# Spreading the maxima of an attention layer over its heads, with stacks of their own, and moving the FFN's low parts to GpSimd

## What is computed

```python
xn = _layernorm(x, axis=-1)
x = x + attn(xn, W_qkv, W_out, rel_emb) + ffn(xn, router_w, w1, b1, w2, b2)

# attn: 16 heads of 16
scores = jnp.einsum('bhqd,bhkd->bhqk', q, k)
scores = scores + compute_bias(rel_emb, S, S)      # bucketed relative position
attn = jax.nn.softmax(scores, axis=-1)
out = jnp.einsum('bhqk,bhkd->bhqd', attn, v)       # then @ W_out

# ffn: F = 1024; top-2 router probabilities, normalised, summed
expert_out = gelu(xt @ w1 + b1) @ w2 + b2
out = expert_out * jnp.sum(combine, axis=-1, keepdims=True)
```

## Time and profile before

| | |
|---|---|
| median of three runs | 3269.54 us (3268.29 to 3270.3) |
| the profiled execution | 3269.68 us, its span 3267.8 us |
| busy: PE, VectorE, ScalarE, GpSimd | 98%, 86%, 75%, 40% |
| chain that ended last: PE, VectorE, DMA | 77%, 3%, 2% |
| stage 1, up to the start of attention | 0 to 594 us |
| attention | 594 to 3199 us |
| projection | 3202 to 3268 us |

### The profile page before, as it was taken

The page is one execution under the profiler, slowest core; times in us unless marked ns, Lnnn a source line. Parts: engine busy times, 40 slices in busy tenths (PEclk is TensorE's granted clock), DMA queues, the critical chain, the costliest instruction groups (busy, mean ns, idle before and its releaser), DMA issues.

```text
span 3267.8 us, 72368 instructions
## 1 busy us (share of the span) xinstructions
PE 3200.7 (98%) x28170; PEld 1717.4 (53%) x28170; DVE 2813.3 (86%) x3760; ACT 2439.0 (75%) x4667; POOL 1297.9 (40%) x1918
## 2 busy tenths in 40 slices
PE   7999999799999999999999999999999999999997
PEld 6888889344444444444444444444444444444446
DVE  5577765699999999999999999999999999999922
ACT  4443344588888888888888888888888888888883
POOL 1212112344444444444444444444444444444445
PEclk9999999899999999999999999999999999999999
DMA  8532232432222222221122222212222221222105
GB/s 194 123 91 78 78 108 87 78 66 37 37 37 37 37 37 37 37 37 37 37 37 37 37 37 37 37 37 37 37 37 37 37 37 37 37 37 37 23 10 186
DMA packets 136725, 175.46 MB, mean 54 GB/s; under 512 B 53008, under 2 KB 100816, under 8 KB 130048
## 3 DMA queue, kind: packets, MB, share of 16 engines
q1 hardware_dynamic: 136384, 170.83, 25.6%
HBM read 110.31 MB, written 56.69 MB: 51 GB/s over the span
## 4 chain that ended last, share of the span: by engine, by line
PE 77%; DVE 3%; DMA 2%; issue 1%; SPq 0%; POOL 0%; ACT 0%; DVEq 0%; ACTq 0%
PE ps L1108 27%; PE ps L1125 24%; PE ps L1097 18%; PE ps L1130 8%; DVE max_half L1042 2%; DMA out_rows<-base_in 1%; PE ps L1165 0%; DMA k_st<-base_in 0%; DMA base_in<-base_rows 0%; SPq L194 0%; POOL prob L1007 0%; DVE neg_turn L1055 0%; SPq L860 0%; POOL turned L1015 0%; ACT turned L967 0%
## 5 line engine op out<-in xcount | busy, mean ns | idle before, releaser
L1042 DVE TENSOR_REDUCE max_half<-ps 128x1 f32<-128x512 f32 (+1 forms) x2666 | 2398.1, 945 | 121.5 <-PE ps L1097 118.1
L960 ACT ACTIVATE prob<-ps 128x512 f32<-128x512 f32 x4096 | 2156.3, 600 | 440.4 <-PE ps L1108 428.4
L1007 POOL TENSOR_TENSOR prob<-prob,near 128x224 f32<-128x224 f32 (+2 forms) x1664 | 978.3, 603 | 1450.9 <-ACT prob L960 1444.6
L1108 PE MATMUL ps<-q_st,k_st 49*128 49x512 f32 x4096 | 1407.3, 442 | 21.4 <-DMA k_st<-base_in 21.1
L1097 PE MATMUL ps<-k_st,q_st 48*128 48x512 f32 x3968 | 1403.2, 450 | 8.5 <-DVE max_half L1042 7.1
L1108 PEld LDWEIGHTS ps<-q_st,k_st 49*128 49x128 f32 x4096 | 658.8, 184 | 747.3 <-ACT prob L960 681.1
L1125 PE MATMUL ps<-prob,vr 128*32 128x384 f32 x4864 | 756.3, 498 | 0.0
L1097 PEld LDWEIGHTS ps<-k_st,q_st 48*128 48x128 f32 x3968 | 636.9, 184 | 180.7 <-DVE max_half L1042 103.3
L1125 PE MATMUL ps<-prob,vx 128*32 128x384 f32 x3328 | 593.5, 499 | 1.1 <-issue 1.1
L1125 PEld LDWEIGHTS ps<-prob,vr 128*32 128x32 f32 x4864 | 133.4, 108 | 325.5 <-issue 221.4
L662 PE MATMUL ps<-xnt,w_parts 128*128 128x512 f32 x1152 | 275.4, 398 | 8.7 <-DVE parts L512 5.1
(11 more groups left out here) (70 smaller groups left out, 1161.6 us busy)
## 6 DMA issues: line engine op xcount, KB each, us to landing
qk_parts<-parts SPq DMA_DIRECT2D x64, 512.0 KB, 4.7
q_st<-qk_parts SPq DMA_DIRECT2D x192, 128.0 KB, 3.9
k_st<-qk_parts SPq DMA_DIRECT2D x192, 128.0 KB, 5.4
near<-bias_near SPq DMA_DIRECT2D x64, 352.0 KB, 6.2
x_sb<-in_L_attn_hidden_states SPq DMA_DIRECT2D x18, 512.0 KB, 6.1
base_rows<-x_sb SPq DMA_DIRECT2D x16, 512.0 KB, 2.9
recip_rows<-recip_all SPq DMA_DIRECT2D x256, 32.0 KB, 1.8
base_in<-base_rows SPq DMA_DIRECT2D x16, 512.0 KB, 5.7
```

The costliest lines, as they stand in the source:

```text
L960: nc.scalar.activation(prob[:, t % PROBS, CH * j:CH * (j + 1)], ps[:, bank_of(at)], ACT.Exp).then_inc(drained, 1)
L1007: nc.gpsimd.tensor_tensor(at, at, near[n % GROUP][:, side, c0:c0 + q1 - q0], ALU.mult).then_inc(near_done, 1)
L1042: nc.vector.tensor_reduce(max_half[:, m % 2].rearrange("p i c -> p (i c)")[:, k:k + len(banks)], tiles, AX.X, ALU.max) \
L1108: nc.tensor.matmul(ps[:, bank_of(at)], k_st[u][:, P * kb:P * (kb + 1)], q_st[u][:, CH * c:CH * (c + 1)], start=True, stop=True).then_inc(s ...
```

## The change

Four things are changed.

1. **The stream of maxima.** The 62 heads' 3968 tiles are no longer tied to "two heads ahead, one for each score tile". `max_groups` spreads them evenly over the 4010 tile places of heads 0 to 62 (without the last 8 visits of head 62). A visit takes as many as the running share says: mostly as many as it has score tiles, in 42 visits one fewer. The maxima of head m so end at visit 22, 44, 66 ... and later by and by: for head 41 at visit 9 of head 40, for head 63 at visit 13 of head 62. `combine` comes one visit later and `turn` two visits later. Scores use 3 banks to the end.
2. **Stacks.** There are two for scores and two for maxima. Q and K of a head are loaded twice: `load(n+1)` at the start of head n, `load_max(m)` after the maxima of head m - 2. SyncE's queue for a head has a new order.
3. **Early pieces.** All 64 are in batch 1, 16 in each chunk: 3 in the QK part, 4 in F1, 1 in VR, 8 in F2, these last in banks 4 and 5.
4. **FFN low parts** are made by GpSimd (`hid_lows`), with `norm` ahead of the fourth of them and `exps` behind the eighth.

```diff
+VISIT_OF = [v for v, visit in enumerate(VISITS) for _ in visit]
+SPARE = 8
...
 def max_groups():
...
+    wanted, slots = CPB * KB * (NH - EARLY_HEADS), CPB * KB * (NH - 1) - sum(len(visit) for visit in VISITS[NV - SPARE:])
+    passed = done = 0
+    for t in range(NV * NH):
+        passed = min(passed + len(VISITS[t % NV]), slots)
+        take = wanted * passed // slots - done
+        tiles = []
+        while take > 0:
+            m, k = EARLY_HEADS + done // (CPB * KB), done % (CPB * KB)
+            size = min(take, 2, CPB * KB - k)
...
+            if k + size == CPB * KB:
+                ends[m] = t, at
...
+TURN_LATER = 2
...
+                def hid_lows(n):
+                    for f in range(KF):
+                        if f == 3:
+                            norm(n + 1)
+
+                        wait(pool, hid_high, KF * n + f + 1)
+                        if f == 0:
+                            wait(pool, f2_ready, TPC * n)
+                        nc.gpsimd.tensor_tensor(hid[:, 1, f], hid_raw[:, f % RAWS], hid[:, 0, f].bitcast(F32), ALU.subtract).then_inc(hid_low, 1)
...
-                for b in range(1, B - 1):
+                for b in range(1, B):
                     for c in range(CPB):
-                        chunk(b, c, early=True)
-                for c in range(CPB):
-                    chunk(B - 1, c, last=c == CPB - 1)
+                        chunk(b, c, early=b <= EARLY_PASSES, last=b == B - 1 and c == CPB - 1)
...
+                def load_max(m):
+
+                    if m - STACKS >= EARLY_HEADS:
+                        sp.wait_ge(max_ready, max_end(m - STACKS))
+                    load_stacks(sp, m, q_max[m % STACKS], k_max[m % STACKS], max_in[m % STACKS])
+
+                def load_maxima(first, last):
+
+                    for m in range(EARLY_HEADS + STACKS, NH):
+                        if first <= MAX_ENDS[m - STACKS][0] < last:
+                            load_max(m)
...
+                def turned_in(n):
+
+                    return MAX_ENDS[n][0] + TURN_LATER if n >= EARLY_HEADS else 0
+
                 def shift(n):
 
-                    wait(sp, neg_turned, n + 1)
+                    wait(sp, score_ready, CPB * KB * (n - STACKS + 1))
+                    sp.wait_ge(neg_turned, n + 1)
...
                 for n in range(NH):
-                    if n + GROUP - 1 < NH:
-                        load(n + GROUP - 1)
-                        load_near(n + GROUP - 1)
+                    early_turn = n + 1 < NH and turned_in(n + 1) < NV * n
                     if n + 1 < NH:
+                        load(n + 1)
+                    if early_turn:
                         shift(n + 1)
+                    load_maxima(NV * (n - 1) + NORM_AT, NV * n)
+                    if n + NEARS - 1 < NH:
+                        load_near(n + NEARS - 1)
                     if n > 0:
                         totals(n - 1)
                         spread(n - 1)
+                    load_maxima(NV * n, NV * n + TOTAL_AT)
+                    if n > 0:
                         keep(n - 1)
+                    load_maxima(NV * n + TOTAL_AT, NV * n + NORM_AT)
+                    if n + 1 < NH and not early_turn:
+                        shift(n + 1)
```

More of the change, by code:

```diff
@@ L132 @@
 NEAR_UP_TO = [sum(len(visit_parts(visit)) for visit in VISITS[:v]) for v in range(NV + 1)]
+VISIT_OF = [v for v, visit in enumerate(VISITS) for _ in visit]
+SPARE = 8
 def max_groups():
     freed = {bank: bank - CPB for bank in range(CPB)}
[L138 to L156, removed]
+    groups, order, in_visit, ends = [], {}, [], {}
+    wanted, slots = CPB * KB * (NH - EARLY_HEADS), CPB * KB * (NH - 1) - sum(len(visit) for visit in VISITS[NV - SPARE:])
[7 more added lines that the diff above has]
+            size = min(take, 2, CPB * KB - k)
+            at = len(groups)
+            choices = [range(bank, bank + size) for bank in range(CPB + 1 - size)]
+            banks = min(choices, key=lambda taken: sorted((freed[bank] for bank in taken), reverse=True))
+            for i in sorted(range(size), key=lambda i: freed[banks[i]]):
+                tiles.append((m, k + i, banks[i], freed[banks[i]], at))
+            for bank in banks:
+                freed[bank] = at
+            groups.append((m, k, banks))
+            if k + size == CPB * KB:
+                ends[m] = t, at
+            done += size
+            take -= size
+        in_visit.append(tiles)
+    assert done == wanted
+    return groups, in_visit, ends
+MAX_GROUPS, MAX_IN_VISIT, MAX_ENDS = max_groups()
+TURN_LATER = 2
 def bucket_line():
@@ L513, in chunk @@
                             .then_inc(lo_done, 1)
[L514 to L515 removed]
+                        if early and m in EARLY_QK:
+                            early_max(b, c, EARLY_QK[m])
                     if not first:
@@ L533, in chunk @@
                             w_low_part(W_2)
+                        if early and f in EARLY_F1:
+                            early_max(b, c, EARLY_F1[f])
+                    if early:
+                        early_max(b, c, EARLY_VR[1])
                     wait(dve, r_copied, TPC * (n + 1))
@@ L700, in chunk @@
                             .then_inc(f1_ready, 1)
+                        if early and f in EARLY_F1:
+                            early_scores(b, c, EARLY_F1[f])
                     for t in range(TPC):
@@ L710, in chunk @@
                             .then_inc(vr_ready, 1)
+                        if early and t in EARLY_VR:
+                            early_scores(b, c, EARLY_VR[t])
                     if early:
-                        wait(pe, max_done, early_first(b, c) + 1)
+                        wait(pe, max_done, early_first(b, c) + EARLY_F2)
                     transposes(n + 1)
@@ L1091, in _, with maxima @@
             def _(pe):
[L1092 to L1094 removed]
+                def maxima(m, k, bank, before, at, last):
+                    if MAX_GROUPS[at][1] == 0:
+                        pe.wait_ge(max_in[m % STACKS], 16 * STACK_LOADS * ((m - EARLY_HEADS) // STACKS + 1))
                     wait(pe, max_done, EARLY + before + 1 if before >= 0 else 0)
[L1096 to L1098 removed]
+                    mm = nc.tensor.matmul(ps[:, MAX_BANK + bank], query_block(q_max[m % STACKS], k // CPB),
+                                          k_max[m % STACKS][:, CH * (k % CPB):CH * (k % CPB + 1)], start=True, stop=True)
                     if last:
```

244 lines of the change are left out of this document (117 added, 127 removed).

## The result

The changed kernel takes 3571.93 us (median of four runs, 3558.29 to 3583.69) beside 3269.65 us of the kernel before, measured with it: a ratio of 1.092 (95% interval 1.088 to 1.097), or 302 us more. Slower was forecast, but as +133 us; the range ended at 3465. The profiled execution took 3558.29 us, its span 3556.5 us, which is 289 us more than the span of before. That difference is what is taken apart here. It is the fastest of the four executions; the others took 7 to 25 us longer, at a mean granted clock of 0.940 to 0.945 instead of 0.949, and what they spent it on isn't on record.

A forecast was written before the change was run, and what follows sets the result against it. Attention was taken as bound by the maxima on VectorE, loosely followed by PE and ScalarE, the FFN stage by PE. 3269.7 us +24 +95 +4.6 +1 +2 +8 -1.2 (+133.4) gave 3403 us, range 3315 to 3465.

The forecast's parts named there:

- Part 2, the short delay: Head starts: shift, queued behind `keep`, 0.8 us late for PE; net +0.6 each, 24 us for 40 heads.
- Part 3, the late heads: Heads 40 to 60: six stack loads ahead of the shift; net +4.5 us each, 95 us (67 to 128).
- the six alone I estimate to be through 6.0 us after their first issue, and the shift about 1.2 us behind them: Late heads: six stack loads through at 1863.7, the shift landed at 1864.9, so 4.2 us late.
- The prediction's upper bound: Late heads: +6.1 us each, with last landing 4.8 us behind its issue, lower clock added, less the stream.
- The lower clock: Late heads: after PE's gap, half of an estimated 1.3 us for a few slower visits, so 0.6 us.
- 4.1 lies between: PE's 4.1 us standstill in late heads lies between gaps of 2.20 (clock 0.98) and 5.16 us (clock 0.50).
- The third rival: Every late head starts at the lower clock, first visits stretch normalisation too: +1.5 us each, 3434 us; chance 0.12.
- Parts 4 and 5, stage 1: FFN: lows on GpSimd, +2 us; 16 early pieces a chunk in batch 1, +8; start of attention, -1.2.
- The fourth rival: FFN: GpSimd's subtractions and `add_base` hold each other up over 16 chunks: +31 us, 3433 us; chance 0.08.
- Part 1, the stream: Attention: 42 visits each spare VectorE a reduction, 27.7 us at most; summed only as 0.2 and 0.35 a head.
- the first rival: Head starts: shift lands before PE wants it, VectorE's saving counts in full: 3254 us, faster; chance 0.07.
- Head 62 and three banks: Head 62's chain takes 41.4 us, +4.6; three score banks in the last 30 visits, 1 us in all.

The follow-up runs named there:

- experiment 4: Changed kernel with three Q loads ahead of the shift and the three K loads behind it in late heads: 3461.7 us, 1.059.
- experiment 3: Changed kernel plus 28 matmuls that nobody reads, ahead of PE's wait for the shift in heads 41 to 61: 3510.73 us, 1.074.
- experiment 7: Changed kernel with the shift ahead of `keep`, and `norm` ahead of the third low part instead of the fourth: 3278.32 us, 1.003.
- experiments 8 and 9: Changed kernel, shift ahead of `keep`, stage 1 of before: 3260.8 us, 0.998; then the same with maxima tied to places as before: 3269.7 us, 1.001.
- experiment 2: Changed kernel with the shift issued ahead of `keep` for every head: 3287.79 us, 1.006.

## Why the prediction was wrong

**What bounds the kernel: right.** Attention was bound by VectorE with PE just behind. But the reserve behind it was taken too large, see the stream below.

**Part 2, the short delay: right.** +0.8 us a head instead of +0.6. The shift lands 1.7 us after its issue (1.9 was taken).

**Part 3, the late heads: mechanism and place right, size wrong, and this is what failed.** +10.7 us a late head were measured (51.51 for heads 40 to 60, less 40.77), +4.5 net forecast. Term by term, on means of these 21 heads:
- The shift's issue behind six loads: 2.8 forecast, 3.0 measured.
- From the last issue to the next head: 2.43 us in early heads, 6.62 in late ones, +4.2 where +0.7 was forecast. The step that failed is "the six alone I estimate to be through 6.0 us after their first issue, and the shift about 1.2 us behind them". In the late head of the timeline above, the last of the six to land was in 9.4 us after their first issue (2845.6 less 2836.2), and the last shift DMA 1.8 us behind it (2847.4). The prediction's upper bound took a landing of 4.8 us from shifts of before; 5.7 was measured. (That bound's own terms add up to 6.6 us, not 6.1: 1867.1 less 1860.7, plus 0.6, less 0.35.) With 3.0 us behind three loads (experiment 4), the landing grows with what stands ahead.
- The lower clock: +0.6 forecast, 2.7 us by the later normalisation alone (33.08 into the head instead of 30.39), 3.4 by experiment 3 (51.51 less 48.14). The step "4.1 lies between" 2.20 and 5.16 rested on a gap that was too small. With gaps of 6.7 to 8.4 us the clock went to 0.50 at each late start, for 7 to 24 us. Nor does 2.20 mark a safe gap: at the starts of heads 8, 19, 23 and 33 of after, PE stood idle 2.5, 1.9, 2.3 and 1.5 us, and the clock then was 0.50 for 3 to 10 us. The third rival, every late head at the lower clock, was right in kind; with the 0.6 of the forecast and its own 1.5 it had 2.1 us a head. The sentence of the Trainium skill (TensorE: Matmul & The Clock Gate, on HAM oscillation), that idle gaps between bursts of matmuls send the clock back and that this can recur at each burst, agrees with the trace: 0.67 over 7.6 us behind a gap of 7.75.

The terms feed each other: late landing makes the gap, the gap lowers the clock, and the low clock makes normalisation, `keep` and the next shift late (experiment 3 takes out the clock, and normalisation is back at 30.2). The sum had the clock only as a small addition. Two of the three had been sized from rows of other conditions, and both errors had the same sign.

**Parts 4 and 5, stage 1: +26.1 instead of +8.8.** A subtraction on GpSimd takes 1.33 us (1.24 forecast, 1.4 named as the limit). What was missing is what it does to VectorE: `add_base` 1.9 times, scalings 2.8 times as long. The fourth rival named `add_base` and gave it 31 us; it took the price as if it fell on the path in all chunks. In plain chunks it doesn't: with `norm` one low part sooner `add_base` is still slow and the 0.87 us are gone (experiment 7). The prediction took 0.2 us there, between bounds of 0 and 1.1, and for gelus that come late. The path that cost the time is another: `norm`, the slow scalings, PE's wait for `xn`. In the 16-piece chunks PE stood idle some 3.4 us (13.5 over the four) instead of 2. The Trainium skill (GPSIMD Engine Reference, Specifications) gives the contention for VectorE instructions with two SBUF inputs and for those in a 2-port performance mode; the prediction used the first case alone. `add_base` agrees with it (479 to 914 ns). The scalings, which have one SBUF tensor and two columns of scalars, were hit harder, 407 to 1146 ns; whether they ran in such a mode no run shows.

**Part 1, the stream: too much.** At most 27.7 us, counted in full in the first rival. Measured: 9 us between experiments 8 and 9. VectorE wins 0.66 us at a spared reduction and waits about 0.3 us longer for PE there; what eats the rest was not followed. In the forecast itself it hardly counted, since the shift decided.

**Head 62 and three banks: right.** 40.4 us for head 62 where 41.4 followed from the forecast, head 63 +0.8 where 1 was taken.

**The direction: right for the reason given (the shift comes too late).** The first rival, shift in time, is what experiment 2 makes true by hand: 3287.8 us, where its sum had 3254; the gap is about the stream's missing 19 us and stage 1's 17.

## What to carry to other kernels

Follow a small DMA that an engine waits for through its queue: what matters is what is issued ahead of it, issue time and transfers both; here what came behind cost nothing. Where a new wait makes PE idle, price the clock that falls after it and the work that the slow stretch delays in turn, and go round the loop once more before you add up. Work moved to GpSimd is not free on VectorE: look at what VectorE does at that time with data in SBUF, and keep short GpSimd steps that others wait for ahead of the long ones.

## What the runs showed of the hardware that wasn't expected

- The last head ran at a granted clock of 0.50 for 55 to 65 us in several profiles, while PE's rows left no idle time. It costs some 24 us (36 us become 60). What starts it, and why it lasts, was not found.
- Scalings on VectorE with one tensor in SBUF (407 ns) took 1146 ns beside GpSimd's subtractions, longer by more than `add_base` with two (479 to 914 ns); the reduction from PSUM was untouched (1222 and 1225 ns).
- A shift DMA of 2 KB, which lands in 1.7 us behind the `keep` DMAs alone, landed 3.0 us after issue behind 384 KB of loads and 5.7 us behind 768 KB of the same queue. With none of these loads ahead, 12 behind it made no difference (1.7 us).
